# Column sums of the edge attributes as an extra product column, and layer normalisation on rows centred by a product, in a graph-network kernel

## The reference

```python
e = relu(bn(edge_attr @ ee_w1 + ee_b1)) @ ee_w2 + ee_b2   # bn: mean and variance over all edges
h = h + segment_sum(e, dst)
z = h + segment_sum(h[src], dst)
z = relu(bn(z @ mlp_w1 + mlp_b1))                         # bn over all nodes
z = relu(bn(z @ mlp_w2 + mlp_b2))
out = layernorm(x + z)        # per row: (v - mean) / sqrt(var + 1e-5)
```

## Time and profile before

| | |
|---|---|
| median of 3 runs | 2282.17 us (2281.79 to 2283.35) |
| the profiled execution | 2281.99 us, of which 2280.2 us are the span that the trace covers |
| PE busy | 2106.6 us, 92% of the span |
| DVE busy | 1833.7 us, 80% |
| POOL busy | 1648.8 us, 72% |
| ACT busy | 1000.2 us, 44% |
| moved by transfers | 174.97 MB |

### The profile page before, as it was taken

How to read it: one execution, slowest core, us unless ns; L and a number is a source line. 1 busy time by engine, 2 the same in 40 slices (tenths; PEclk the granted TensorE clock), 3 DMA queues, 4 the chain that set the end, 5 groups by cost and what they waited for, 6 DMA issues and landing times. The chain is left out here.

```text
span 2280.2 us, 57729 instructions
## 1 busy us (share of the span) xinstructions
PE 2106.6 (92%) x15974; PEld 1659.1 (73%) x15974; DVE 1833.7 (80%) x3770; ACT 1000.2 (44%) x1753; POOL 1648.8 (72%) x1645
## 2 busy tenths in 40 slices
PE   5699999999975999999999999999999999999873
PEld 5699999999943777777777777777777777777532
DVE  7799999999997777777777777777777777777578
ACT  0022222222253555555555555555545545555476
POOL 3188888888867777777777777777777777777213
PEclk7799999999997999999999999999999999999985
DMA  6433333333362211111111111111111111112015
GB/s 199 138 107 101 102 109 101 103 108 101 92 203 66 54 54 54 53 54 54 53 54 54 53 54 54 53 54 54 53 54 54 53 54 54 53 54 54 22 42 183
DMA packets 86254, 174.97 MB, mean 77 GB/s; under 512 B 36619, under 2 KB 38171, under 8 KB 85893
## 3 DMA queue, kind: packets, MB, share of 16 engines
q1 hardware_dynamic: 46086, 97.33, 14.1%
q0 software_dynamic: 36608, 75.05, 11.9%
q10 hardware_dynamic: 3407, 1.21, 0.3%
HBM read 160.67 MB, written 12.80 MB: 76 GB/s over the span
## 5 line engine op out<-in xcount | busy, mean ns | idle before, releaser
L805 POOL DMA_INDIRECT table<-h_scratch,idx x1144 | 1079.6, 944 | 353.9 <-issue 348.3
L934 DVE TENSOR_TENSOR table<-ps,keys 128x480 bf16<-128x480 f32 x1300 | 816.7, 653 | 14.1 <-PE ps L827 11.9
L840 PE MATMUL ps<-table,counts_even 128*128 128x384 bf16 x2600 | 530.2, 327 | 0.0
L840 PE MATMUL ps<-table 128*128 128x384 bf16 x2600 | 528.1, 326 | 0.0
L893 ACT CAST counts_even<-ps 128x480 bf16<-128x480 f32 x650 | 363.4, 559 | 366.4 <-PE ps L827 364.6
L893 ACT CAST table<-ps 128x480 bf16<-128x480 f32 x650 | 363.4, 559 | 351.2 <-PE ps L827 350.1
L827 PE MATMUL ps<-table 128*128 128x240 bf16 x2600 | 480.6, 267 | 27.5 <-DVE table L934 22.9
L585 PE MATMUL ps<-table 128*128 128x96 f32 x3328 | 414.5, 278 | 0.0
L585 PEld LDWEIGHTS ps<-table 128*128 128x128 f32 x3328 | 388.6, 192 | 0.0
L827 PEld LDWEIGHTS ps<-table 128*128 128x128 bf16 x2600 | 253.2, 101 | 183.0 <-DVE table L934 41.6
L852 PEld LDWEIGHTS ps<-table 128*128 128x128 f32 x2288 | 278.4, 192 | 59.9 <-issue 52.6
(11 more groups left out here) (151 smaller groups left out, 1399.5 us busy)
## 6 DMA issues: line engine op xcount, KB each, us to landing
table<-in_edges_t SPq DMA_DIRECT2D x416, 128.0 KB, 2.5
table<-h_scratch,idx POOLq DMA_INDIRECT x1144, 2.5
table<-in_edges SPq DMA_DIRECT2D x26, 512.0 KB, 4.5
table<-in_x_t SPq DMA_DIRECT2D x48, 256.0 KB, 2.9
h_scratch<-table SPq DMA_DIRECT2D x24, 256.0 KB, 2.0
out<-table SPq DMA_DIRECT2D x24, 256.0 KB, 2.0
table<-in_dst_groups SPq DMA_DIRECT2D x1, 832.0 KB
table<-in_dst_mixed SPq DMA_DIRECT2D x1, 832.0 KB
```

The lines of the kernel that those rows point to most:

```text
L805: pool.indirect_dma_start(near_rows[:, u, t * D:(t + 1) * D], None, h_dram, bass.IndirectOffsetOnAxis(ap=idx[:, v, at + t:at + t + 1], axis=0)
L840: mm = pe.matmul(ps[:, PACK_BANKS[v], 0:SPLITS * D], counts[(v * LISTS + c) % 2][:, b, :], h_split[:, j * SPLITS * D:(j + 1) * SPLITS * D] ...
L934: dve.tensor_tensor(match[:, k], ps[:, 0, 0:LIST_COLS].unsqueeze(1).broadcast_to([P, 2, LIST_COLS]), keys[:, v, c, 2 * k:2 * k + 2].unsque ...
```

## The change

In the prologue each block of 128 columns gets a 129th column that POOL sets to one at the start (`gram_rows`: four slots of eight blocks of 129 columns). The product with the 129 columns as the moving side leaves the sums of the 128 columns in column 128 of the same bank. DVE's 26 sums, the sum over the pieces and the wait for `gram_summed` go away; a copy of that PSUM column (`column_sums`) and two small products with `fold` give the 16 means. A gram load now writes eight pieces of 512 bytes per partition, 516 bytes apart, instead of 4 KB in a row. The work on `wide`, `base` and `rel` moves from the end of DVE's program to the place right behind the indices; PE's two products for it stand before the last two gram loads. The copy of `iota` moves into a wait for ACT's root. The product and the addition for `per_edge` move into the h stage, to the head of PE's and DVE's programs there.

In the layer normalisation the turn by the identity becomes a product with `center` (identity minus 1/128 everywhere), so that the rows come out centred. ACT squares a chunk from PSUM into SBUF, DVE sums the squares per row in one instruction and takes the reciprocal of ACT's root, and one DVE instruction per chunk scales all four rows. `bn_stats`, `bn_aggr`, the shift and ACT's scaling are gone. DVE scales three chunks behind its sum.

```diff
-                sp.dma_start(rows[:, s, 0:GRAM_COLS],
-                             a["edges"][:, bass.ds(n * GRAM_COLS, GRAM_COLS)]).then_inc(gram_in[s], 16)
+                sp.dma_start(gram_rows[:, s, :, 0:P],
+                             a["edges"][:, bass.ds(n * GRAM_COLS, GRAM_COLS)].rearrange("p (b w) -> p b w", w=P)
+                             ).then_inc(gram_in[s], 16)
             def reload(s, i):
                 sp.wait_ge(gram_done, i * GRAM_SLOTS + (s + 1 - GRAM_SLOTS))
-                sp.wait_ge(gram_summed, i * GRAM_SLOTS + (s + 1 - GRAM_SLOTS))
                 load(s, i * GRAM_SLOTS + s)
...
+            pool.memset(gram_rows[:, :, :, P:], 1.0).then_inc(ones_set, 1)
...
-                    x = rows[:, s, b * P:(b + 1) * P]
-                    mm = pe.matmul(ps[:, 0, 0:P], x, x, start=(n == 0 and b == 0), stop=True,
-                                   skip_group_check=True)
+                    mm = pe.matmul(ps[:, 0, 0:P + 1], gram_rows[:, s, b, 0:P], gram_rows[:, s, b, :],
+                                   start=(n == 0 and b == 0), stop=True, skip_group_check=True)
...
-            pe.matmul(ps[0:1, 1, 0:ED], ones[:, 0:1], part1, start=True, stop=True)
-            pe.matmul(ps[0:ED, 2, 0:1], part1, ones[:, 0:1], start=True, stop=True)
...
+            pe.matmul(ps[0:1, 1, 0:ED], column_sums, fold[:], start=True, stop=True)
+            pe.matmul(ps[0:ED, 2, 0:1], fold[:], column_sums, start=True, stop=True)
...
+            link(dve.tensor_copy(column_sums, ps[:, 0, P:P + 1]))
...
             # h stage
             def turn_h(c, s, n):
                 pe.wait_ge(h_ready, c + 1)
+                pe.wait_ge(edge_made, 2)
...
+            pe.matmul(ps[:, 7, 0:1], ee_w2[:], shift_col[:], start=True, stop=True).then_inc(edge_made, 1)
             lagging(pe, [project, between, turn_h], slots=8)
...
+            dve.wait_ge(edge_made, 1)
+            dve.tensor_tensor(per_edge[:], ps[:, 7, 0:1], colvec[:, 0:1], ALU.add).then_inc(edge_made, 1)
...
             # layer normalisation
-                turn(pe, s, summed[:, s % 2, :], n).then_inc(turned2, 1)
+                for k in range(PER):
+                    mm = pe.matmul(ps[0:n // PER, s, k * D:(k + 1) * D], summed[:, s % 2, k:n:PER], center[:],
+                                   start=True, stop=True)
+                mm.then_inc(centered, 1)
...
+                dve.wait_ge(squared, c + 1)
+                dve.tensor_reduce(ln_squares[0:q, s, :], by_row(squares[0:q, s % 4, :]), AX_X, ALU.add
+                                  ).then_inc(measured, 1)
...
+                dve.tensor_tensor(by_row(staged_out[0:q, s % 4, :]), by_row(ps[0:q, s, :]),
+                                  ln_rstd[0:q, s, :].unsqueeze(2).broadcast_to([q, PER, D]), ALU.mult
+                                  ).then_inc(normed, 1)
 
-            lagging(dve, [measure, aggregate, between, between, invert_and_shift, normalize], BANKS)
+            lagging(dve, [measure, between, invert, normalize], BANKS)
...
+                act.wait_ge(centered, c + 1)
+                wait(act, measured, c - 3)
+                act.activation(squares[0:q, s % 4, :], ps[0:q, s, :], ACT.Square).then_inc(squared, 1)
...
-            lagging(act, [relu] + 3 * [between] + [root] + 2 * [between] + [normalize], BANKS)
+            lagging(act, [relu, between, between, square, between, root], BANKS)
```

More of the change, by code:

```diff
@@ L325, in link @@
                     dve.wait_ge(step, steps[0])
[L328 to L332, removed]
-                for s in range(GRAM_SLOTS):
-                    sum_slot(s, 0)
                 dve.wait_ge(groups_in, 32)
@@ L360, in _ @@
                 dve.tensor_reduce(wide[0:HALVES, 3:4], most_mixed[:], AX_X, ALU.max).then_inc(spread, 1)
-                with dve.Fori(1, GRAM_BODIES) as i:
-                    for s in range(GRAM_SLOTS):
-                        sum_slot(s, i)
-                for s in range(GRAM_REST):
-                    sum_slot(s, GRAM_BODIES)
-                dve.wait_ge(gram_summed, GRAM_LOADS)
-                link(dve.tensor_reduce(part1, part.rearrange("p n c -> p c n"), AX_X, ALU.add))
+                dve.wait_ge(wide_ready, 1)
+                dve.tensor_scalar(wide[:, 1:2], ps[:, 6, 0:1], 0.5, None, ALU.is_ge).then_inc(spread, 1)
+                dve.wait_ge(spread, 4)
+                dve.tensor_scalar(wide[:, 2:3], wide[:, 1:2], -1.0, 1.0, ALU.mult, ALU.add).then_inc(spread, 1)
+                dve.tensor_scalar(rounds_i[:], wide[0:1, 1:2], float(ROUNDS_ALL - 1), 1.0, ALU.mult, ALU.add)
+                dve.wait_ge(base_in, 16)
+                dve.wait_ge(spread, 5)
+                for first, last, width in ((DENSE_AT, BASES, NARROW), (GROUPS, DENSE_AT, NEAR), (0, GROUPS, WINDOW)):
+                    ins = dve.tensor_scalar(base[:, first:last], base[:, first:last], wide[:, 2:3], float(width),
+                                            ALU.mult, ALU.subtract)
+                ins.then_inc(spread, 1)
+                dve.wait_ge(spread, 6)
+                in_groups = rel[:, 0:TILES].rearrange("p (g t) -> p g t", t=GROUP_TILES)
+                dve.tensor_tensor(in_groups, in_groups,
+                                  base[:, 0:GROUPS].unsqueeze(2).broadcast_to([P, GROUPS, GROUP_TILES]), ALU.subtract)
                 dve.wait_ge(gram_done, GRAM_LOADS)
@@ L381, in _ @@
                 dve.wait_ge(pe_step, 4)
+                dve.tensor_copy(ps[:, 5, 0:WINDOW], iota)
                 dve.wait_ge(root_ready, 1)
@@ L1148, in _, with by_row @@
+                over_chunks(pe, center_rows, slots=BANKS)
             @block.vector
             def _(dve):
+                def by_row(v):
+                    return v.rearrange("p (k d) -> p k d", k=PER)
                 def measure(c, s, n):
                     q = n // PER
-                    dve.wait_ge(turned2, c + 1)
-                    for k in range(PER):
-                        ins = dve.bn_stats(ln_parts[0:q, s, k, :], ps[0:q, s, k * D:(k + 1) * D])
-                    ins.then_inc(ln_stat, 1)
@@ L1175, in normalize @@
                 def normalize(c, s, n):
[L1177 to L1178 removed]
                     q = n // PER
[L1180 removed]
+                    dve.wait_ge(inverted, c + 1)
                     dve.wait_ge(out_done[s % 4], uses(c, s % 4, 4) + 16)
[L1182 to L1185 removed]
```

106 lines of the change are left out of this document (31 added, 75 removed).

## The result

| | before | changed |
|---|---|---|
| median | 2281.98 us (2281.55 to 2283.35, 4 runs) | 2260.68 us (2259.38 to 2261.82, 4 runs) |
| the profiled execution, its span | 2281.99, 2280.2 us | 2261.45, 2259.7 us |
| PE, DVE, ACT busy | 2106.6, 1833.7, 1000.2 us | 2122.8, 1762.0, 993.1 us |

A forecast was written before the change was run, and what follows sets the result against it. DVE was taken to bound the layer normalisation and, through its late column sums, the gram loads. -14.0 - 4.3 - 12.0 = -30.3 us from 2281.99 gave 2251.7 us (2252 against the median), range 2244 to 2269.

The forecast's parts named there:

- the gram loads: Prologue: last gram product at 67.2 us instead of 81.2, at 1.85 us per load: -14.0 us.
- the layer normalisation: Final stage: 1.8 us per chunk instead of 2.4, last store at 2260.9 us instead of 2272.85: -12.0 us.
- the chain: Prologue, small steps behind the last gram product: -5.2 us, -4.3 together with the later h stage.
- the h stage: Its first DVE step waits for PE's product and an addition moved there: +0.9 us.
- the case of dear pieces: Gram loads: 512-byte pieces at 2.65 us per load, time 2269.3 us; chance 0.14.
- I add 1 us for the first wave's dearer pieces: Gram loads: second wave of products starts at 23.2 us instead of 22.23, +1 us.
- the cover: Prologue: `wide`, `base` and `rel`, 3.6 us, run hidden beside the last two gram loads, 3.7 us.
- PE: eight records, 0.86 us warm, 1.72 us cold: Layer normalisation: PE's centring time per chunk, at full and at half clock; at most 1.75 us even cold.
- Short pieces at 2.65 us: Rival, gram loads: a queue full of short pieces takes 2.65 us per load, time 2269.3 us; chance 0.14.
- the slower case: Gram loads: pieces at 60 ns, 3.84 us per load, products end at 111.0 us, time 2295.5 us; chance 0.07.
- POOL's block: Rival, layer normalisation: POOL's add delays DVE's sums, pace 2.1 us, 2259.1 us; chance 0.16, including that pace for another reason.
- the prologue's pace doesn't change: Rival: transfers hold gram loads to 1.88 us, only the index-work wait goes, 2252.4 us; inside the first case, no separate chance.

## Why the prediction was right, and what in it was not

The way and the mechanism were right: DVE let go of SP in the prologue and was no longer the bound in the layer normalisation. The sum was not, by 9.8 us in the profiled executions: 5.9 in the gram loads, 2.2 in the window sums, 1.7 in the layer normalisation and 1.1 in the stages between, less 1.1 from the chain and the h stage. The time lies inside the range because that reached up to 2269 us for the case of dear pieces, which didn't happen; that part is luck.

**The gram loads.** SP no longer waits for DVE, as predicted. The pace of 1.83 us per load is the 1.85 that was taken, but by luck: the pieces were to set it through the transfers, and with whole pieces it is 1.80 us, so PE does. That PE could go at 1.70 was a misreading: the earlier trace rows counts 47 records in 5 us with those that only reach into the stretch (one lasts 275 ns), while the earlier trace rows has 225 in 25.44 us, 113 ns each. PE took 1.81 us a load before the change as well.

The term that failed is "I add 1 us for the first wave's dearer pieces". It was 4.6 us: the second wave starts at 26.80 for 22.23 us. SP took 4.50 us to issue the four loads that took 1.94 in whole pieces, and the indices came later: DVE's first step on them begins at 22.85 us, with whole pieces at 19.08. But SP's time isn't what held the wave: the load that begins it is issued at 9.27 us, with whole pieces at 8.91, and its products start 17.5 us behind that for 13.8. The time passes in the queue, behind the first loads and the indices; with pieces of 1 KB, which SP issues in 2.21 us, the second wave still starts 2.0 us later than with whole ones. What in the queue takes it stays open. The rest is 2.1 us of waits behind the second wave. I had counted the half clock there as 3.3 us lost; what the traces point to is that full slots stop the transfers: in the execution whose wave was 1.5 us shorter the products ended no earlier. The run with whole pieces ends at 67.15 us, the time predicted for the short ones.

**The price of a piece.** Packets of q1 from 45 to 60 us of the changed kernel, of the kernel with 1 KB pieces and of the one with whole pieces: count, MB, share of 16 engines.

```profile
q1 hardware_dynamic: 8368, 4.22, 110.1%
```

```profile
q1 hardware_dynamic: 4260, 4.23, 90.2%
```

```profile
q1 hardware_dynamic: 1210, 4.39, 85.6%
```

Over 16 engines and 15 us these are 31.6, 50.8 and 169.8 ns. 26 ns had been taken for the first, 41.5 was the upper bound. Eight short ones take 253 ns against 170 for one whole. These are the packets' own times. The first share is over 100%, so packets overlap there, and what a piece costs a full queue isn't shown. Since PE was the bound, the steady part did not pay for it. The Trainium skill (DMA: Bandwidth & Descriptors, Why small descriptors are slow) gave an estimate of 216 ns by its fixed charge; by the packets' own times the sign agrees, and the size isn't tested.

**The chain behind them.** 6.0 us for 5.2. The two small products left uncounted are 0.5 us of it: the third product of the means now starts 0.16 us behind the first (73.83 and 73.67 us), before 0.63 (83.18 and 82.55). The steps on `wide`, `base` and `rel` end at 72.79 us, before the last product at 73.09, so the cover holds. The h stage is 0.6 us late instead of 0.9.

**The window sums** had no term; the late clock took 2.2 us there, and with the clock kept up they come back. Whether the change makes a late rise likelier stays open.

**The layer normalisation.** DVE's sum and scaling take 686 and 659 ns, as said, and POOL's addition beside them blocks neither: no sum of the 25 took more than 689 ns, and that rival falls.

```profile
L1146 DVE TENSOR_REDUCE ln<-table x25: 668/686/689, 2205.4 to 2249.5; 128x4 f32<-128x512 f32 x24, 53x4 f32<-53x512 f32 x1
```

The Trainium skill (SBUF — State Buffer, Who interferes with whom) says that a `tensor_reduce` never contends with GpSimd on this chip; these 689 ns agree.

The pace was 1.8 us taken and 1.865 measured, but again for another reason. The step that failed is "PE: eight records, 0.86 us warm, 1.72 us cold": they take 1.865 us at full clock (eight of 233 ns), because the stationary columns lie 16 bytes apart, and that set the pace. The prediction's price for PE came from the gram products, whose columns are neighbours. ACT, the transfers and the order on SP, which I had named, lie behind: without the stride the stage is 5.3 to 5.9 us shorter, with transfers at 309 GB/s. The Trainium skill (SBUF — State Buffer, Door 1: The DMA port swizzle) says that SBUF is read in lines of 16 bytes and that an access which goes to a new line each time pays. At a stride of four fp32 columns that is every one, and the runs agree: 330 for 192 ns. The same passage of the Trainium skill gives four fp32 as how far one can stride for free; here that stride was not free, and the measurement decides.

The end was mis-sized too: the scaling of four chunks still stands behind the last sum in DVE's order, and from the end of that sum to the last store it is 2.9 us instead of 1.5. Last store: 54.9 us behind the first relu, where 52.6 had been predicted; 1.6 of these 2.3 us are the pace.

**Rivals.** Short pieces at 2.65 us, the slower case and POOL's block didn't happen. The time lies near the one given for POOL's block (2259.1) by coincidence. That the prologue's pace doesn't change is what came about, though not through the transfers: 1.81 us a load before and 1.83 behind it; what went is the wait for the index work.

## What to carry to other kernels

When a stage's bound is taken away, price the next engine with the operands it will have, strides included: a product's weight load with a stride of 16 bytes took 1.7 times as long here, and letting the engine that writes the operand lay it out cost nothing (1258 ns for 1248). When a load is cut into short pieces, ask what stands behind it at the head of a queue: there the pieces delayed the next wave by some 4 us, while in the steady part another engine hid them. Take an engine's pace from many records in a row, not from a count in a short stretch. And check where a moved stage meets the clock: 16 idle products in a wait ahead of it were worth 2.8 us in the stage's own time against a late rise, 0.7 against an early one.

## What the hardware showed that I had not expected

The rise of the granted clock behind a wait differs between executions of the same code: 4.7 us behind PE's first record in one and 9.3 us in the other, worth 2.1 us in a stage of 521. What decides it stays open.

PE's clock in the layer normalisation stood at 1.00 with products, PE busy for 25 of 25 us, where it had been 0.50 with turns by the identity, busy for 18.79 of 40 us. A run that tells turns from products at the same load was not made.

The stride cost nothing at half clock. At the start of the stage, with the clock at 0.50, the weight loads take 329 ns (median) with the stride and 333 ns with neighbouring columns:

```profile
L1133 PEld LDWEIGHTS ps<-center_sb,summed x20: 308/329/332, 2202.5 to 2206.9; 128*128 128x128 f32 x20
```

```profile
L1133 PEld LDWEIGHTS ps<-center_sb,summed x16: 288/333/333, 2203.8 to 2207.0; 128*128 128x128 f32 x16
```

With neighbouring columns the full clock brings 192 ns; with the stride they stay at 330.

The turns of before took the same stride, and their weight loads are 217 ns on average, at half clock, not 323. A turn has one record in the trace and a product two. Why a turn pays less is open.

SP's time to issue a load hardly depends on its pieces, but at the head of the queue it grows: over all 26 loads the median is 378 ns with pieces of 512 bytes and 333 ns with whole ones, the longest 11.85 us and 0.55 us.

```profile
L218 SPq DMA_DIRECT2D table<-in_edges x26: 372/378/11848, 0.7 to 65.3; - x26
```

```profile
L218 SPq DMA_DIRECT2D table<-in_edges x26: 332/333/547, 0.7 to 59.6; - x26
```

So the 4.50 us for the first four loads (1.94 in whole pieces, 2.21 at 1 KB) are no price per load: the same issue takes 0.38 us later on. What holds SP there no run shows.
